# A graph layer on one core: Pool writes a scrap of 128 columns between one gather of x rows and the next, from the ninth gather on

## What is computed

```python
h = jnp.maximum(_layernorm(x, axis=-1), 0.0)
msg = jax.nn.relu(h[src] + edge_attr_256)              # 25000 x 256
p = msg @ W_fc.T + b_fc                                # 25000 x 256
scores = p @ Q.T                                       # 4 heads
alpha = w / jnp.maximum(denom[dst], 1e-09)             # w: softmax of the scores over each node's edges
pooled = [segment_sum(alpha[:, h:h + 1] * p, dst) for h in range(4)]
gate = softmax(mean_p @ Wg.T + bg)                     # mean_p: mean of p over each node's edges
out = x + sigmoid(einsum('nh,nht->nt', gate, pooled))  # 50000 x 256
```

## Time and profile before

| | us |
|---|---|
| runs, without a trace | 659.47, 658.44, 654.64 |
| median | 658.44 |
| span of the profiled execution, first to last instruction | 732.9 |

### The profile page before, as it was taken

One profiled execution on the slowest core, in us unless ns is written; L12 is line 12 of the kernel. 1 busy time (PEld: TensorE's weight loads), 2 busy tenths in 40 slices (PEclk: granted clock), 3 DMA queues, 4 the chain that ended last, 5 costly groups with the idle time before them and its releaser, 6 DMA issues.

```text
span 732.9 us, 12416 instructions
## 1 busy us (share of the span) xinstructions
PE 548.9 (75%) x2474; PEld 434.1 (59%) x2475; DVE 487.6 (67%) x1644; ACT 383.3 (52%) x661; POOL 453.4 (62%) x339
## 2 busy tenths in 40 slices
PE   2417988878779868879403998888888778877785
PEld 2205876666558656758202876776667566665564
DVE  4208678788879768769798766666565655555555
ACT  2105455656457545647211254666666666666674
POOL 7765565665560656550053366777877887778785
PEclk9999899999999999989855999999999999999999
DMA  7434455555553468775300799999999999999999
GB/s 223 131 93 134 147 173 174 165 174 154 174 170 114 129 224 271 237 234 191 115 0 1 247 355 383 314 307 329 357 319 329 325 327 339 325 337 336 341 333 332
DMA packets 137238, 171.53 MB, mean 234 GB/s; under 512 B 10096, under 2 KB 123784, under 8 KB 137202
## 3 DMA queue, kind: packets, MB, share of 16 engines
q10 hardware_dynamic: 91344, 90.23, 37.6%
q1 hardware_dynamic: 33010, 42.70, 18.6%
q0 software_dynamic: 12848, 38.20, 16.5%
HBM read 111.50 MB, written 59.60 MB: 233 GB/s over the span
## 4 chain that ended last, share of the span: by engine, by line
PE 52%; issue 12%; ACT 11%; DVE 10%; another core or an unknown queue 5%; ACTq 4%; DVEq 3%; POOL 2%; DMA 2%; POOLq 0%; SPq 0%
PE bank L745 24%; PE bank L829 18%; PE bank L735 7%; ACT arena L597 5%; DVE spread L1248 3%; ACT bank L573 3%; POOL arena L478 2%; ACTq L600 2%; DVEq L1252 1%; ACT arena L505 1%; ACTq L552 1%; ACTq L605 1%; ACT arena L497 1%; DMA p_keep<-p_spill 1%
## 5 line engine op out<-in xcount | busy, mean ns | idle before, releaser
L829 PE MATMUL bank<-p_keep,spread 128*128 x1172 | 274.1, 388 | 51.6 <-DVE spread L1248 46.7
L829 PEld LDWEIGHTS bank<-p_keep,spread 128*128 128x128 f32 x1172 | 219.0, 192 | 107.5 <-issue 79.8
L1248 DVE TENSOR_SCALAR spread<-bank,rel,wgt 128x128 f32<-128x128 f32 x586 | 195.8, 404 | 128.5 <-PE bank L829 72.8
L478 POOL TENSOR_TENSOR arena<-arena 128x1024 f32<-128x1024 f32 x96 | 224.9, 2352 | 73.1 <-ACT arena L597 72.7
L745 PE MATMUL bank<-w_all,arena 128*128 128x264 f32 (+1 forms) x784 | 228.0, 417 | 53.2 <-ACT arena L505 40.2
L745 PEld LDWEIGHTS bank<-w_all,arena 128*128 128x128 f32 (+1 forms) x784 | 143.7, 204 | 78.9 <-ACT arena L505 50.9
L597 ACT ACTIVATE arena<-bank 128x1024 f32<-128x1024 f32 x97 | 99.2, 1023 | 139.3 <-PE bank L829 120.3
L443 POOL DMA_INDIRECT p_keep<-in_x_dram,idx x124 | 120.8, 975 | 72.6 <-issue 31.5
L505 ACT ACTIVATE arena<-bank 128x256 f32<-128x256 f32 x196 | 73.6, 376 | 124.2 <-PE bank L735 71.0
L443 POOL DMA_INDIRECT arena<-in_x_dram,idx x72 | 70.1, 973 | 64.7 <-ACT arena L497 33.7
L573 ACT ACTIVATE bank<-zero 128x1024 f32<-128x1024 f32 x98 | 100.5, 1026 | 3.0
(11 more groups left out here) (202 smaller groups left out, 190.6 us busy)
## 6 DMA issues: line engine op xcount, KB each, us to landing
out_dram<-arena ACTq DMA_DIRECT2D x97, 512.0 KB, 4.5
arena<-in_x_dram ACTq DMA_DIRECT2D x73, 512.0 KB, 5.4
arena<-in_edge_attr_dram SPq DMA_DIRECT2D x48, 512.0 KB
arena<-in_x_dram POOLq DMA_DIRECT2D x24, 512.0 KB, 5.8
p_spill<-p_keep SPq DMA_DIRECT2D x16, 512.0 KB
p_keep<-p_spill SPq DMA_DIRECT2D x16, 512.0 KB, 5.8
p_keep<-in_x_dram,idx POOLq DMA_INDIRECT x124
arena<-in_x_dram,idx POOLq DMA_INDIRECT x72
```

The costliest lines, as they stand in the source:

```text
L478: pool.tensor_tensor(yout[:, slot, :, :], yout[:, slot, :, :], xin[:, slot, :, :], ALU.add).then_inc(summed, 1)
L829: nc.tensor.matmul(places[:, bass.ds(place, T)], spread[:, k0 + k, :], p_rows[:, bass.ds(p_at, T)], start=False, stop=True, skip_group_che ...
L1248: v.tensor_scalar(spread[:, k, :], bank[:, 7, P:2 * P], rel[:, bass.ds(s0 + k, 1)], wgt[:, bass.ds(s0 + k, 1)], ALU.is_equal, ALU.mult).th ...
```

## The change

Pool gets a further tile, `pause`, of 128 x 128 float32, which nothing reads, and a semaphore `paused`. Behind every gather from `t = 8` on (`FIRST` is 8) Pool clears it with a memset. Each memset but the first waits until the memset before it is done. The first eight gathers stand as they were.

```diff
+        pause = sb("pause", [P, P])
...
+        paused = sem("paused")
...
                 pool.indirect_dma_start(out=x_row(t), out_offset=None, in_=x,
                                         in_offset=bass.IndirectOffsetOnAxis(ap=idx[0:rows_of(t), t:t + 1], axis=0),
                                         ).then_inc(gathered[k], 16)
+                if t >= FIRST:
+                    if t > FIRST:
+                        pool.wait_ge(paused, t - FIRST)
+                    pool.memset(pause[:, :], 0.0).then_inc(paused, 1)
```

## The result

The changed kernel takes 671.24 us (median of 4 runs, 668.79 to 676.98) and the kernel before, on the same chip, 656.54 us (4 runs, 654.18 to 659.47). By the medians the change is slower by 14.7 us, by the interval of the ratio 12.5 to 19.2 us, where the prediction said slower by 41.1. The profiled execution of the changed kernel took 673.32 us, its span 671.6 us; between an execution's time and its span lie 1.7 us in every run that follows.

What follows compares the result with a forecast made beforehand. Pool's gathers, 1.26 us a tile, were taken to bound the gather stage in timed runs. 187 memset rounds x 0.22 us = 41.1 us, added to 658.4, gave 699.6 us; own range 679 to 722, wide range 640 to 735.

Steps and rivals of the forecast that it cites:

- Pool's bare pace: Gather stage: one gather each 1.26 us with nothing to wait for, plus a 21.8 us tail, ends at 271.7 us.
- I take it that the stalls come with the tracing: Gather stage: timed runs lack the traced stalls; stage at most 277.9 us there, against 352.4 us traced.
- the faster case: Gather stage: timed runs have stalls too and the pause breaks them; 619 us, or 639 with half; chance 0.20.
- The memset and its place: Pool: 188 memsets of about 0.20 us, each within 0.02 us of its gather's end.
- The wait at nothing: Pool: each memset's wait for the one before, a whole gather ahead, costs nothing.
- The 0.30 us before a gather: Pool's "issue" idle stays whole behind the memset, so a round becomes 1.48 us, 0.22 more than 1.26.
- The bound at the low end: Pool's extra per round is 0 if the 0.30 us before a gather runs beside the memset.
- the hidden pause: Pool: preparation runs beside the memset, or pauses lie in Pool's waits; no change, 658 us; chance 0.14.
- The gathers' own brakes don't bind at this pace: Gather stage: the gathers' own brakes don't bind at the changed kernel's pace of 1.48 us a round.
- Nothing hides it: TensorE's 1.11 us a tile: Gather stage: TensorE's 1.11 us a tile is already below Pool's 1.26, so nothing hides the added 41.1 us.
- Costly wait: Pool: the pause costs its wait as well, 187 x 0.46 = 86 us, so 744 us; chance 0.08.
- broken stalls: Gather stage: the pause breaks stalls present in timed runs, faster by over 1%, 619 to 639 us; chance 0.20.

Runs made afterwards that it cites:

- second trace: The kernel before, unchanged, profiled again: 657.96 us (one execution), span 656.3 us, gather stage ending at 273.2 us.
- the earlier trace: First profiled execution of the kernel before, unchanged, with stalls on every engine: span 732.9 us, gather stage ending at 352.4 us.
- the scraps: Kernel before, no pause on Pool, VectorE clearing a scratch tile once a tile: 64 columns 655.91 us (0.9963), 256 columns 690.16 us (1.0501), 1 column 656.18 us (0.9965).

## Why the prediction was right in its direction and wrong in its size

**What bounds the stage: right.** Pool's gathers set the end of the stage in the timed runs. The unchanged kernel's second trace has its stage at 273.2 us, where the prediction had 271.7 by Pool's bare pace. The agreement is better than its parts and in so far luck: the last gather is at 257.3 and not at 249.9, mostly since 28 of the gathers last over 1.1 us instead of 0.96, and the tail behind it is 15.9 us and not the 21.8 of the earlier trace rows, which came from the stalled execution. "In the first 54 us no engine but Pool does much" came from there too; TensorE is busy 43.20 us of them in the second trace.

**"I take it that the stalls come with the tracing": right in what was drawn from it, wrong as to the cause.** The timed runs have no such stalls, so the faster case (619 to 639 us) had no ground. But tracing alone isn't it, since the trace of the unchanged kernel at 657.96 us has none either. Nor do the stalls "belong to Pool's unbroken runs of gathers": that trace is one such run from first to last. What stalled the one execution stays open. The page "Runtime: NRT & Kernel Launch" (The launch sequence) of the Trainium skill puts a profile's total some 6 us above the timed execution whatever the kernel. No run here shows that total. Each execution's own time is 1.7 us above its span, so the 74.5 us between the earlier trace rows and the median were never an overhead of either kind, but another execution.

**The memset and its place: right.** 188 memsets, 0.22 us instead of 0.20, each at once behind its gather.

**The wait at nothing: right**, shown by the first two rounds of the changed kernel, one without a wait and one with it (1.34 and 1.33 us), and by the kernel without it (1.0014 beside 1.0026).

**The 0.30 us before a gather: the step that failed.** "I take 0.22, since both of its parts have a row of their own and the hiding has none." The term was 0.02 + 0.20 with the whole 0.30 us still behind it. Measured: 0.22 + 0.16 in place of 0.30, so 0.08 us a round. 0.14 us of what stood as idle time before a gather runs beside the instruction ahead of it. The sum with the measured term is 187 x 0.08 = 15.0 us in place of 41.1; 656.5 + 15.0 = 671.5 us, and the median is 671.24. The bound at the low end had named this mechanism, all of the 0.30 us hidden; the truth lies between, closer to that bound, and below the 679 us at which the forecast's own range ended. That the wide range from 640 to 735 holds it is no merit of the forecast's term: it was made to hold the hidden pause as well.

The rows could have said more. In the earlier trace rows the load that starts 0.30 us after an addition is released by "POOL arena L478": it waits for the addition itself. In the earlier trace rows the releaser is "issue": the gather waits for nothing on Pool. The first row may hold the passing of a signal from the addition as well as the start of the load, so it is weak evidence that 0.30 us must follow an instruction that isn't waited for. This is a reading and not shown: the load without its wait wasn't tried.

**"The gathers' own brakes don't bind at this pace": right but for one wait**, the 1.86 us before the gather at 161.17 us, whose cause is open. Besides the three brakes named, the gather of tile 108 also waits for a table that TensorE adds up; it has 0.16 us before it in the changed kernel, as others have.

**"Nothing hides it: TensorE's 1.11 us a tile": right for TensorE, but the next engine is VectorE.** With fewer gathers it takes 1.22 us a tile, and the stage ends only 7.4 us earlier; the scraps put its room at no more than some 12 us. For a change that makes Pool slower this mattered little. For one that makes it faster it sets the most that can be had, about 8 us here.

**The rivals.** Hidden pause: two thirds of it were true, 0.14 of the memset's 0.22 us. Costly wait and broken stalls: fallen, the latter also by the pause of one column, which brings no relief (1.0026).

## What to carry to other kernels

Idle time marked "issue" before an instruction need not be a price that is added to whatever is put in front of it: here part of it ran beside that. So take the new distance between the two old neighbours as max(idle, new + rest), where the rest lies anywhere from nothing to the whole idle time while no row shows it, and don't put the forecast at one end. Before a profile's span is used for a sum, set it against the median; an execution that is 74 us off is another execution, and should be replaced by one that agrees before the length of a stage is taken from it. What a change of the slowest engine can bring is shown by the distance to the next one, which is found by taking work off the slowest, or by adding work to the next until the time moves. Where an engine's records overlap, the cost of an instruction is the shift of the starts behind it, not its duration.

## What the runs showed of the hardware that was not expected

Of the 0.30 us between two gathers on Pool, 0.14 us overlap a memset that stands between them; with a memset of 0.12 us the gap that is left is 0.19 us, and from 0.17 us on it is 0.16. Pool's memset on 128 partitions takes 0.12, 0.17, 0.22 and 0.33 us for 1, 64, 128 and 256 columns: 0.12 us and about 0.08 us for each 100 columns. On VectorE a memset of 64 columns has a record of 112 ns and moves the instructions behind it by some 20 ns; one of 256 columns has a record of 272 ns and moves them by 220 ns. Behind both, the records of other instructions are shorter, the statistics in the mean 393 ns instead of 418 and the small addition 110 instead of 166, where behind one of 1 column they aren't; which property of the neighbour does it wasn't tried.
